# An expert stage reordered by token half, Q evictions split by section, and the gate's low half transposed by DMA

## The reference

```python
# attention: xn = layernorm(x)
scores = einsum('bsd,de,bte->bst', xn, qk, xn) / 32      # causal
x = x + einsum('bst,btd,de->bse', softmax(scores), xn, ov)
# experts: xt = layernorm(x), 1024 wide, INTER 512, 16 experts, top 4 of 2 groups
c = gate weights, (tokens, 16), zero where not chosen
y = einsum('tei,eid,te->td', silu(xt @ w1[e]) * (xt @ w3[e]), w2, c)
z = silu(xt @ ws1) * (xt @ ws3) @ ws2                    # shared, inner width 1024
x = x + y + z
```

## Time and profile before

| | us |
|---|---|
| median of 3 runs | 2682.83 (2681.56 to 2960.99) |
| the profiled execution | 2690.57 |
| its span on the slowest core | 2688.7 |
| spans of the eight cores | 2667.8 to 2688.7 |
| TensorE busy | 2206.8 (82%) |
| VectorE busy | 1096.9 (41%) |
| ScalarE busy | 574.6 (21%) |
| expert stage, from its first weight load to its last matmul | 1150.6 to 2684.3 |

### The profile page before, as it was taken

One profiled execution on the slowest core, in us unless ns is written; L12 is line 12 of the kernel. 1 busy time (PEld: TensorE's weight loads), 2 busy tenths in 40 slices (PEclk: granted clock), 3 DMA queues, 4 the chain that ended last, 5 costly groups with the idle time before them and its releaser, 6 DMA issues.

```text
span 2688.7 us, 32703 instructions; the slowest of 8 cores (2667.8 to 2688.7 us)
## 1 busy us (share of the span) xinstructions
PE 2206.8 (82%) x10595; PEld 992.2 (37%) x10800; DVE 1096.9 (41%) x1615; ACT 574.6 (21%) x885; POOL 32.9 (1%) x66
## 2 busy tenths in 40 slices
PE   0441989898887652189999999999999999999999
PEld 0110444443443221134444444444444444444443
DVE  3213546465566525523342334323433233432333
ACT  2323344344354423310001100011000100011000
POOL 0000000000000000000000000000000000000000
PEclk9876999999998875599999999999999999999999
DMA  7213212222234422122212022120221212221203
GB/s 144 66 43 90 71 36 78 65 64 79 78 80 111 110 60 45 31 55 40 47 34 45 17 48 48 32 48 16 48 48 32 39 25 47 48 32 22 42 1 125
DMA packets 129743, 147.05 MB, mean 55 GB/s; under 512 B 104240, under 2 KB 108592, under 8 KB 122928
## 3 DMA queue, kind: packets, MB, share of 16 engines
q0 software_dynamic: 11936, 60.98, 12.4%
q1 hardware_dynamic: 117648, 83.97, 12.0%
HBM read 172.36 MB, written 8.39 MB: 67 GB/s over the span
## 4 chain that ended last, share of the span: by engine, by line
PE 55%; DVE 1%; issue 1%; DVEq 0%
PE H L892 37%; PE H L918 18%; DVE APR L906 1%; DVE ACC L929 0%; DVE ACC L935 0%; DVEq L113 0%
## 5 line engine op out<-in xcount | busy, mean ns | idle before, releaser
L892 PE MATMUL H<-XF,W1B 128*128 128x512 bf16 x2259 | 519.2, 380 | 17.0 <-PEq L118 14.7
L918 PE MATMUL H<-W2B,APR 128*128 128x512 bf16 x2256 | 503.1, 378 | 32.9 <-DVE APR L906 29.2
L892 PE MATMUL H<-XF,W3B 128*128 128x512 bf16 x2258 | 517.0, 379 | 2.4
L906 DVE TENSOR_TENSOR APR<-SCRF,H 128x1024 bf16<-128x1024 f32 x144 | 175.8, 1221 | 824.0 <-PE H L892 824.0
L902 ACT ACTIVATE SCRF<-H 128x1024 f32<-128x1024 f32 x144 | 147.4, 1023 | 1347.2 <-PE H L892 1347.2
L929 DVE SCALAR_TENSOR_TENSOR ACC<-H,CC,ACC 128x1024 f32<-128x1024 f32 x256 | 328.5, 1283 | 148.3 <-PE H L918 147.9
L892 PEld LDWEIGHTS H<-XF,W1B 128*128 128x128 bf16 x2304 | 224.8, 98 | 289.5 <-issue 23.1
L918 PEld LDWEIGHTS H<-W2B,APR 128*128 128x128 bf16 x2304 | 207.0, 97 | 329.0 <-issue 118.8
L892 PEld LDWEIGHTS H<-XF,W3B 128*128 128x128 bf16 x2304 | 225.4, 98 | 271.8
L515 PE MATMUL PS_PV<-VP,PTS 128*128 128x512 bf16 x1059 | 260.4, 399 | 19.2 <-DVE ACC L527 8.6
L255 DVE TENSOR_SCALAR_CACHE_REDUCE XLNBF<-STG 128x1024 bf16<-128x1024 f32 x80 | 97.3, 1216 | 187.1 <-DMA STG<-x_own 111.2
(11 more groups left out here) (113 smaller groups left out, 1064.4 us busy)
## 6 DMA issues: line engine op xcount, KB each, us to landing
STG<-x_seq SPq DMA_DIRECT2D x64, 512.0 KB, 3.8
W1B<-w_img POOLq DMA_DIRECT2D x16, 1024.0 KB, 8.0
W3B<-w_img POOLq DMA_DIRECT2D x16, 1024.0 KB, 9.4
W2B<-w_img POOLq DMA_DIRECT2D x16, 1024.0 KB, 8.3
STG<-x_own SPq DMA_DIRECT2D x16, 512.0 KB, 5.1
XOWNF<-x_own SPq DMA_DIRECT2D x16, 512.0 KB, 3.7
out<-ACC SPq DMA_DIRECT2D x16, 512.0 KB, 2.6
OVB<-ov_img POOLq DMA_DIRECT2D x1, 2048.0 KB, 20.0
```

The costliest lines, as they stand in the source:

```text
L892: wbuf=wbuf, ich=ich, th=th, pi=pi: t.matmul(ps[:, half * 512:(half + 1) * 512], wbuf[:, pi * 4096 + dch * 512 + ich * 128: pi * 4096 + dc ...
L906: lambda v, h3ps=h3ps, ich=ich, th=th: v.tensor_mul(APR[:, ich * NT + th * TCH: ich * NT + (th + 1) * TCH], SCRF32[:, 0:TCH], h3ps[:, 0:TCH]),
L918: t.matmul(yp[:, half * 512:(half + 1) * 512], APR[:, ich * NT + tt * 128: ich * NT + (tt + 1) * 128], W2B[:, pi * 4096 + ich * 1024 + hal ...
```

## The change

Three edits.

1. Q stage: the eviction of a group with odd g is issued on VectorE (`tensor_scalar_mul`) and not on ScalarE.
2. Gate stage: XLO is transposed by a DMA from SP into a new tensor XLOT (128 x 2048, bf16) and not by TensorE and ScalarE. The DMA uses the stream that the tile's XF transpose doesn't use.
3. Expert stage: the loops are exchanged. th is the outer loop and ich the inner one, and the 8 W2 groups of a token half follow directly on its four W1/W3 pairs. The pair of PSUM tensors is picked by (th * 4 + ich) % 2.

```diff
-                    P.emit("scalar", lambda s: s.activation(
-                        qsl(ech, sg * 512, 512), bank[:, 0:512], AF.Identity,
-                        scale=CONST[:, 0:1]),
-                        reads=[rbank, rCONST], writes=[rQ], inc="sc")
+                    if g % 2 == 0:
+                        P.emit("scalar", lambda s: s.activation(
+                            qsl(ech, sg * 512, 512), bank[:, 0:512], AF.Identity,
+                            scale=CONST[:, 0:1]),
+                            reads=[rbank, rCONST], writes=[rQ], inc="sc")
+                    else:
+                        P.emit("vector", lambda v: v.tensor_scalar_mul(
+                            qsl(ech, sg * 512, 512), bank[:, 0:512],
+                            CONST[:, 0:1]),
+                            reads=[rbank, rCONST], writes=[rQ], inc="ve")
...
+        XLOT = s2.enter_context(nc.sbuf_tensor("XLOT", [128, 2048], BF16))
+            rXLOT = [R("xlot0"), R("xlot1")]
...
-                    fns = [(lambda t, dch=dch, lane=lane: t.transpose(
-                        PT2B[:, dch * 128:(dch + 1) * 128],
-                        xlo(lane)[:, dch * 128:(dch + 1) * 128], IDB[:, :]))
-                        for dch in range(8)]
-                    P.group("tensor", fns, reads=[rXLO[lane], rIDB],
-                            writes=[rPT2B], inc="pe")
-                    P.emit("scalar", lambda s, lane=lane: s.copy(
-                        xlo(lane), PT2B[:, :]),
-                        reads=[rPT2B], writes=[rXLO[lane]], inc="sc")
+                    sTP[(m + 1) % 2].issue(lambda s, lane=lane: s.dma_start(
+                        XLOT[:, lane * D:(lane + 1) * D]
+                        .rearrange("p (c q) -> p c q", q=128),
+                        xlo(lane)[:, :].rearrange("p (c q) -> p c q", q=128),
+                        transpose=True),
+                        reads=[rXLO[lane]], writes=[rXLOT[lane]])
...
-                    P.group("tensor", fns, reads=[rXF, rXLO[lane], rGW],
+                    P.group("tensor", fns, reads=[rXF, rXLOT[lane], rGW],
                             writes=[rpg], inc="pe")
...
-                    for ich in range(4):
-                        for th in range(NTH):
-                            hp = (ich * NTH + th) % 2
+                    for th in range(NTH):
+                        for ich in range(4):
+                            hp = (th * 4 + ich) % 2
...
-                    for tt in range(NSLOT):
-                        yp, ryp = HH[tt % 2], rH[tt % 2]
...
+                        if th == NTH - 1:
+                            for tt in range(8 * th, NSLOT):
+                                w2_tt(tt)
+                        else:
+                            for tt in range(8 * th, 8 * (th + 1)):
+                                w2_tt(tt)
```

More of the change, by code:

```diff
@@ L764, in fn @@
                                     lhs = (xf(dch, m * 128, 128) if sn == "hi"
-                                           else xlo(lane)[:, dch * 128:(dch + 1) * 128])
+                                           else XLOT[:, lane * D + dch * 128:
+                                                     lane * D + (dch + 1) * 128])
                                     return t.matmul(
@@ L880, in do_expert, with w2_tt @@
                         prefetch_expert(e + 1, 1 - pi)
-                    for ich in range(4):
-                        for th in range(NTH):
-                            hp = (ich * NTH + th) % 2
+                    def w2_tt(tt):
+                        yp, ryp = HH[tt % 2], rH[tt % 2]
+                        fns = []
+                        for ich in range(4):
+                            for half in range(2):
+                                fns.append(
+                                    lambda t, ich=ich, half=half, tt=tt, yp=yp,
+                                    pi=pi: t.matmul(
+                                        yp[:, half * 512:(half + 1) * 512],
+                                        APR[:, ich * NT + tt * 128:
+                                            ich * NT + (tt + 1) * 128],
+                                        W2B[:, pi * 4096 + ich * 1024 + half * 512:
+                                            pi * 4096 + ich * 1024 + (half + 1) * 512],
+                                        start=(ich == 0), stop=(ich == 3)))
+                        P.group("tensor", fns, reads=[rAPR, rW2[pi]], writes=[ryp],
+                                inc="pe")
+                        if e < NEXP:
+                            P.emit("vector",
+                                   lambda v, tt=tt, yp=yp, e=e: v.scalar_tensor_tensor(
+                                       acc(tt), yp[:, :],
+                                       CC[:, tt * 16 + e: tt * 16 + e + 1],
+                                       acc(tt), ALU.mult, ALU.add),
+                                   reads=[ryp, rCC], writes=[rACC[tt]], inc="ve")
+                        else:
+                            P.emit("vector", lambda v, tt=tt, yp=yp: v.tensor_add(
+                                acc(tt), acc(tt), yp[:, :]),
+                                reads=[ryp], writes=[rACC[tt]], inc="ve")
+                        if e == NEXP + 1:
+                            sSO[tt % 4].issue(lambda s, tt=tt: s.dma_start(
+                                out_d[tt], acc(tt)),
+                                reads=[rACC[tt]])
+                    for th in range(NTH):
+                        for ich in range(4):
+                            hp = (th * 4 + ich) % 2
                             pairs = ((HH[2 * hp], rH[2 * hp], W1B, rW1[pi]),
@@ L910, in do_expert @@
                                    reads=[rSCR[0], rh3], writes=[rAPR], inc="ve")
-                    for tt in range(NSLOT):
-                        yp, ryp = HH[tt % 2], rH[tt % 2]
[L913 to L933, removed]
-                        else:
[L935 to L941, removed]
+                        if th == NTH - 1:
+                            for tt in range(8 * th, NSLOT):
+                                w2_tt(tt)
+                        else:
+                            for tt in range(8 * th, 8 * (th + 1)):
+                                w2_tt(tt)
                 for e in range(NEXP + 2):
```

## The result

The changed kernel takes 2723.22 us and the kernel before, measured beside it, 2684.06, as medians of all executions. The ratio is 1.0139, with a 95% interval of 1.0126 to 1.0151: 1.4% slower, which is clear of the noise but inside the 2% band. The step is 37.9 us, where 38 was forecast.

The account below looks back on a forecast made before the run. The prediction took TensorE's expert matmuls (W1/W3 and W2) as the chain that bounds the kernel, with a wait for APR once per expert. Terms of 32 + 4 + 2 = +38 us moved the median from 2682.83 to 2721, range 2702 to 2740.

Parts of the forecast that it names:

- The expert term: Expert stage: 18 more W3-to-W2 passages, each losing 1.78 us waiting for VectorE's multiply into APR, 32.0 us in all.
- The Q term: Q stage: later start of section 2 plus dearer evictions on VectorE, 3.3 + 0.8, about +4 us, bounds -4 and +5.
- The shift of section 2: Q stage: tile 12's statistics queue behind the moved evictions, delaying tile 14's load and section 2's start by 3.3 us.
- The price of the eviction: Q stage: VectorE's eviction taken as equal to ScalarE's, 684 ns against 0.69 us; the hop adds 0.8 us over 14 waits.
- The 0.09 us each: Q stage: the Trainium skill's PSUM-source costs, 0.66 against 0.57 us per moved eviction, 1.4 us in all; not adopted.
- What I had left out: Q stage: section 2's second group ran at granted clock 0.60; a possible 1.7 us gain was not counted.
- The gate term: Gate stage: moving the low half's transpose to SP's DMA costs +2 us, bounds 0 and +10.
- their removal gains nothing: Gate stage: the removed TensorE transposes and ScalarE copies are not on the path; the period stays 8.27 us.
- The two delays that I had added: Gate stage: tile 0's low half lands later, +1.6 us, and the last tile's gate ends later, +0.4 us.
- A hidden second seam: Expert stage rival: TensorE finds the APR chunk ready, so only 4 + 2 us remain, 2689; 5 in 100.
- ScalarE's relief: Gate stage rival: dropping ScalarE's copies shortens the stage by 16 x 1.0 us, giving 2703; 4 in 100.
- The chain of transposes: Gate stage rival: slow landings make tiles a chain, 11.7 us against 8.27, +52 us, 2773 in all; 6 in 100.

Follow-up runs that it names:

- e_half: The kernel before, order unchanged, with APR tracked as two resources, one per token half: 2654.86 us, ratio 0.9882.
- e_gate_3x: The kernel before with only the gate's low-half transposes moved to DMA, each issued three times in a row: one time, 2754.78 us.
- e_gate_late: The kernel before with only the gate's low-half transposes on DMA, and the first weight prefetch held until tile 1's transposes land: one time, 2691.05 us.

## Why the prediction was right

- **The expert term, 18 x 1.78 = 32.0, measured 31.4** (31.6 alone). 36 waits, 58.3 us in total against "some 58"; 86.7 us per expert, as said. The mechanism is shown from both sides: with the wait for the multiply taken away the old order gains the same 32.0 us (`e_half`), and with all waits gone both orders take the same time. Start-to-start was the right measure: the idle column alone would have given 29.0.
- **The Q term, +4, measured +4.0, but not by my sizes.** The shift of section 2 was right: the gap ahead of it grew by 3.3 us (18.9 to 22.2), by the queue that I had named. The price of the eviction was mis-sized: I took 684 ns from VectorE's reduction, and it is 750 ns; TensorE's idle for it is 1.08 us in the steady groups, where it is 0.98 for ScalarE's. That adds up to 1.4 us for 14 waits where I had 0.8 (which the prediction brings down from 1.0 by a rounding that no row supports). The 0.09 us each, 1.4 in all, that the prediction set aside was the nearer figure. What I had left out came back on the other side: on the core of the page the second group of section 2 ran at a granted clock of 1.00 and took 1.89 and not 3.57 us. From section 2's start to the end the stage was 0.3 us shorter, section 1 was 0.9 longer.
- **The gate term, +2, measured -1.3: a small miss.** The step that failed is "their removal gains nothing": the steady period fell from 8.27 to 8.08, some 2.5 us over the 13 periods between the first tile and the last two. I didn't find what held it; VectorE's next pass started 0.25 us after the LOG copy's start before, and 0.08 after. The two delays that I had added came out at 1.8 against 2, but differently spread: the last two gates +0.9 where I had 0.4 (1136.8 - 1136.54 in the prediction is only 0.3), the first gate +0.9 as a mean where I had 1.6 (the step it names is 1.44). That +0.9 is no constant step of 1.44: SP was held at the first low half for 11.9 and 10.5 us on cores 2 and 3, and for 6.2 to 7.4 on the others, and kernels without the edit differ among themselves by as much (1.5 to 2.7).
- **The sum, partly by luck.** The attention stage, which the forecast leaves alone, took 3.1 us more, and the gate stage 3.3 less than forecast; the two misses cancel. In the runs with the Q edit the attention stage was 770.6 to 774.4, in those without 767.4 to 771.8, with 15 us between the cores of one run. Whether that is an effect stays open.
- **The rivals.** A hidden second seam was excluded by 36 waits. ScalarE's relief gave at most the 2.5 us of the period and not 16. The chain of transposes sets the period when a gate waits some 10 us for them (`e_gate_3x`), and not at 3.3 us. The Trainium skill ("VectorE: DVE Perf Modes", The three transpose paths) gives 1309 ns for one 128x128 block by DMA; an estimate from it, block after block, is 10.5 us for eight, and a pair would not have fitted the period. The trace does not agree with that: both transposes land in 3.3 us each, within one period of 8.08. The page prices a single block; to multiply it by eight was my step.

## What to carry to other kernels

An interchange of loops that adds a passage between a producer and a consumer phase can cost the latency of the last product each time (here 1.78 us for a multiply of 1.22), unless work that doesn't need that product stands in between: count the passages, measure one from start to start, and name the next buffer that the fill uses up (here H0 at tile 2). Before moving work to another engine, ask which buffer or resource makes it serial: here two small edits, the tracking of APR by half and the bank index, gave 32 and 34 us, and the change of the evicting engine cost some 4. When a load is moved, look at what it then collides with.

## What the runs showed of the hardware

- VectorE's scaled copy of 128x512 f32 from PSUM to bf16 takes 750 ns, its reduction of the same shape 684, ScalarE's scaled copy 687.
- Beside three weight loads of 1 MB issued from GpSimd, the issue of a single DMA transpose held SP for 6.2 to 11.9 us over the cores of the changed kernel, with the landing 8.3 to 14.6 us after the issue, and for 12.2 to 15.5 us over those of `e_gate_late`, with the landing after 17.1 to 19.8; the medians are 1.23 and 3.3 us. In the kernel before the slowest high half landed after 8.8 to 12.5 us, so the 9.3 of the earlier trace rows was that of one core and no upper bound.
- Two transposes issued 1.4 us apart from SP land in 3.3 us each (medians of the changed kernel), where one by itself took 3.1 in the kernel before.
